# Expert stages: rows turned three groups ahead of the first products, second products two groups behind, one pipeline over both halves

## The reference

```python
x = hidden_states.reshape(-1, H)                       # 4096 tokens, H = 128
probs = jax.nn.sigmoid(x @ router_w.T + expert_bias)   # 160 experts
top_w, top_idx = jax.lax.top_k(probs, 8)               # 8 experts for each token
top_w = top_w / (jnp.sum(top_w, axis=-1, keepdims=True) + 1e-09) * 2.5
combine = zeros(T, 160).at[arange(T)[:, None], top_idx].set(top_w)
h1 = jax.nn.silu(einsum('th,eih->eti', x, w_gate))     # 128 -> 64 for each expert
routed = einsum('eti,ehi->th', h1 * combine.T[:, :, None], w_down)   # 64 -> 128
shared = jax.nn.silu(x @ w_gate_shared.T) @ w_down_shared.T
return routed + shared
```

## Time and profile before

| | |
|---|---|
| runs | 2842.09, 2843.34, 2848.13 us, median 2843.34 |
| span of the profiled execution (no other time of that execution is recorded) | 2871.3 us |
| PE busy | 2020.4 us (70%) |
| DVE, ACT, POOL busy | 1647.2, 1083.0, 1349.4 us |
| expert stage m: first `up` to last `take_y` | about 931 to 1288 us |
| expert stage n: the same | about 2307 to 2654 us, then gathers to the end |

### The profile page before, as it was taken

One profiled execution on the slowest core, in us unless ns is written; L12 is line 12 of the kernel. 1 busy time (PEld: TensorE's weight loads), 2 busy tenths in 40 slices (PEclk: granted clock), 3 DMA queues, 4 the chain that ended last, 5 costly groups with the idle time before them and its releaser, 6 DMA issues. The chain is left out here.

```text
span 2871.3 us, 44772 instructions
## 1 busy us (share of the span) xinstructions
PE 2020.4 (70%) x15403; PEld 1129.8 (39%) x15403; DVE 1647.2 (57%) x4701; ACT 1083.0 (38%) x2067; POOL 1349.4 (47%) x1372
## 2 busy tenths in 40 slices
PE   5898887887883775665887889888888467766000
PEld 3456455455461554541332333333332255545000
DVE  5457585775777231456776778778783533145222
ACT  0263453444541443340545543443444144443000
POOL 0043166566673444553445531641554444355775
PEclk9899989889995887775777877876876589787555
DMA  9200001000034664554131121121100656565221
GB/s 370 96 1 4 1 6 34 23 11 33 20 130 155 192 206 155 180 180 121 28 88 48 46 76 25 53 69 36 49 29 25 250 179 207 176 188 174 70 60 44
DMA packets 132471, 275.63 MB, mean 96 GB/s; under 512 B 29411, under 2 KB 44387, under 8 KB 127891
## 3 DMA queue, kind: packets, MB, share of 16 engines
q1 hardware_dynamic: 99478, 205.60, 21.7%
q0 software_dynamic: 32768, 67.17, 7.7%
HBM read 146.34 MB, written 125.93 MB: 95 GB/s over the span
## 5 line engine op out<-in xcount | busy, mean ns | idle before, releaser
L1473 POOL DMA_INDIRECT slots_in<-g_xs,g_place x512 | 510.1, 996 | 373.0 <-issue 122.7
L2518 ACT ACTIVATE b_pT<-b_psE 128x512 f32<-128x512 f32 (+3 forms) x768 | 325.6, 491 | 449.6 <-PE b_psE L2415 392.6
L2271 DVE TENSOR_REDUCE b_peak<-b_psM 128x1 f32<-128x512 f32 (+3 forms) x768 | 395.1, 551 | 148.6 <-PE b_psM L2403 91.3
L1498 POOL DMA_INDIRECT r_xs<-slots_out,g_place x336 | 333.3, 992 | 237.2 <-ACT b_pT L2518 98.3
L2400 PE MATMUL b_psM<-b_kS,b_qS 72*128 72x512 bf16 (+3 forms) x768 | 290.1, 412 | 60.6 <-DVE b_peak L2271 29.7
L2415 PE MATMUL b_psE<-b_qS,b_kS 75*128 75x512 bf16 (+3 forms) x768 | 250.5, 402 | 45.0 <-ACT b_pT L2518 38.6
L1498 POOL DMA_INDIRECT g_xs<-slots_out,g_place x176 | 173.0, 983 | 126.1 <-issue 48.0
L2060 DVE COPY m_staged_w<-wgd 128x192 f32 x512 | 98.3, 264 | 230.0 <-PE m_psY L2002 165.7
L2427 PE MATMUL b_psV<-b_pT,b_vb 128*32 128x512 f32 (+3 forms) x1536 | 205.8, 616 | 30.8 <-POOL b_pT L2582 29.5
L2060 DVE COPY n_staged_w<-wgd 128x192 f32 x512 | 97.5, 263 | 216.0 <-PE n_psY L2002 118.6
L2400 PEld LDWEIGHTS b_psM<-b_kS,b_qS 72*128 72x128 bf16 x768 | 84.5, 112 | 263.7 <-DVE b_peak L2271 151.6
(11 more groups left out here) (639 smaller groups left out, 4167.9 us busy)
## 6 DMA issues: line engine op xcount, KB each, us to landing
wgd<-in_w_gdT SPq DMA_DIRECT2D x8, 3840.0 KB, 22.7
slots_in<-g_xs SPq DMA_DIRECT2D x26, 1024.0 KB
m_rows<-slots_in SPq DMA_DIRECT2D x104, 256.0 KB
slots_out<-m_y SPq DMA_DIRECT2D x104, 256.0 KB
n_rows<-slots_in SPq DMA_DIRECT2D x104, 256.0 KB
slots_out<-n_y SPq DMA_DIRECT2D x104, 256.0 KB
b_qS<-q_parts SPq DMA_DIRECT2D x48, 192.0 KB
b_kS<-k_parts SPq DMA_DIRECT2D x48, 192.0 KB
```

The costliest lines, as they stand in the source:

```text
L1473: self.nc.gpsimd.indirect_dma_start(self.G.slots_in[self.h], bass.IndirectOffsetOnAxis(self.G.place[:, TPH * self.h + t, k:k + 1], 0), sel ...
L1498: self.nc.gpsimd.indirect_dma_start(self.rows(i)[:, k, :], None, self.G.slots_out[t // TPH], bass.IndirectOffsetOnAxis(self.G.place[:, t, ...
L2271: nc.vector.reduce_max(to, taking()[:, 0:size], AX.X).then_inc(m_taken, 1)
L2518: nc.scalar.activation(pT[:, e % KEPT, h, q0:HALF], psE[:, j % BANKS, q0:HALF], ACT.Exp, scale=SCALE).then_inc(e_taken, 1)
```

## The change

Only `experts` is touched, and both expert stages use it. New constants: `TURN_AHEAD = 3`, `DOWN_BEHIND = 2`, `HELD = 3`. One loop runs over the 104 groups of both halves. In step n PE does up(n), turn_rows(n+3), down(n-2), and ACT squash(n), take_xT(n+3), take_y(n-2). xT and hT get three buffers (HELD); the PSUM tiles keep two places. SP stores group n-2, then loads group n+7, as far as the transposes have freed a buffer; loads of half 1 begin at step 48 (`crossing`), the wait for its scatters stands before its first load. POOL's pace is taken from `hT_ready` in place of `y_ready`; the scatters are spread so that the last is released at group 46 of 52. The weights' staging on DVE and the sizes of all instructions are unchanged.

```diff
@@ SP
+            def load(n):
+                h, i = divmod(n, HALF_GROUPS)
+                if i == 0:
+                    for b in range(BPH * h, BPH * (h + 1)):
+                        sp.wait_ge(S.scattered[b], 16 * TPB * TOPK)
...
-            for h in range(HALVES):
-                for b in range(BPH * h, BPH * (h + 1)):
-                    sp.wait_ge(S.scattered[b], 16 * TPB * TOPK)
-                for i in range(DEEP):
-                    load(h, i)
-                for i in range(HALF_GROUPS):
-                    if i + DEEP < HALF_GROUPS:
-                        sp.wait_ge(x_turned, h * HALF_GROUPS + i + 1)
-                        load(h, i + DEEP)
-                    store(h, i)
+            loaded, crossing = DEEP, HALF_GROUPS - TURN_AHEAD - 1
+            for n in range(-TURN_AHEAD, GROUPS):
+                if n >= DOWN_BEHIND:
+                    store(n - DOWN_BEHIND)
+                for n_load in range(loaded, min(n + TURN_AHEAD + DEEP + 1, GROUPS if n >= crossing else HALF_GROUPS)):
+                    sp.wait_ge(x_turned, n_load - DEEP + 1)
+                    load(n_load)
+                    loaded = n_load + 1
+            for n in range(GROUPS - DOWN_BEHIND, GROUPS):
+                store(n)
@@ POOL
-                        pool.wait_ge(y_ready, first + done)
+                        pool.wait_ge(hT_ready, first + done)
...
-            spaced(scatter, TPH * TOPK - scatter.sent, 0, 3, 2)
+            left = TPH * TOPK - scatter.sent
+            spaced(scatter, left, 0, 3, lambda n: min(n // 3 * 2, n * (HALF_GROUPS - 2 * TURN_AHEAD) // left))
...
@@ PE
-            for h in range(HALVES):
-                first = h * HALF_GROUPS
-                turn_rows(first)
-                for i, (g, d) in enumerate(order):
-                    up(first + i, g, d, h * DYN_GROUPS)
-                    if i + 1 < HALF_GROUPS:
-                        turn_rows(first + i + 1)
-                    if i:
-                        down(first + i - 1, *order[i - 1])
-                down(first + HALF_GROUPS - 1, *order[HALF_GROUPS - 1])
+            for n in range(TURN_AHEAD):
+                turn_rows(n)
+            for n in range(GROUPS):
+                up(n)
+                if n + TURN_AHEAD < GROUPS:
+                    turn_rows(n + TURN_AHEAD)
+                if n >= DOWN_BEHIND:
+                    down(n - DOWN_BEHIND)
+            for n in range(GROUPS - DOWN_BEHIND, GROUPS):
+                down(n)
@@ ACT
-                if n >= 2:
-                    act.wait_ge(up_done, n - 1)
-                nc.scalar.activation(xT[:, n % 2, :], psX[:, n % 2, :], ACT.Copy).then_inc(xT_ready, 1)
+                if n >= HELD:
+                    act.wait_ge(up_done, n - HELD + 1)
+                nc.scalar.activation(xT[:, n % HELD, :], psX[:, n % 2, :], ACT.Copy).then_inc(xT_ready, 1)
```

More of the change, by code:

```diff
@@ L67 @@
 STAGED = 4
+TURN_AHEAD = 3
+DOWN_BEHIND = 2
+HELD = 3
 RING = 4
@@ L1946, in _, with spaced @@
         def _(pool):
-            def spaced(issue, count, first, transfers, groups):
+            def spaced(issue, count, first, transfers, groups_at):
                 for n in range(0, count, transfers):
-                    done = min(n // transfers * groups, HALF_GROUPS)
+                    done = groups_at(n)
                     if done:
-                        pool.wait_ge(y_ready, first + done)
+                        pool.wait_ge(hT_ready, first + done)
                     issue(min(transfers, count - n))
-            spaced(scatter, TPH * TOPK - scatter.sent, 0, 3, 2)
+            left = TPH * TOPK - scatter.sent
+            spaced(scatter, left, 0, 3, lambda n: min(n // 3 * 2, n * (HALF_GROUPS - 2 * TURN_AHEAD) // left))
             for s in S.scattered[BPH:]:
@@ L1959, in _ @@
                 pool.wait_ge(s, 16 * HALF_GROUPS // DEEP)
-            spaced(lambda count: gather.issue(pool, count), min(TPH, gather.tiles) * TOPK, HALF_GROUPS, 2, 1)
+            spaced(lambda count: gather.issue(pool, count), min(TPH, gather.tiles) * TOPK, HALF_GROUPS, 2,
+                   lambda n: min(n // 2, HALF_GROUPS))
             if out is not None:
@@ L1979, in turn_rows, with up @@
                 last.then_inc(x_turned, 1)
-            def up(n, g, d, ahead):
+            def up(n):
+                h, i = divmod(n, HALF_GROUPS)
+                g, d = order[i]
                 pe.wait_ge(xT_ready, n + 1)
@@ L1985, in up @@
                 if d is not None:
-                    pe.wait_ge(staged, ahead + d + 1)
-                elif n < HALF_GROUPS and GROUP * g % CHUNK == 0:
+                    pe.wait_ge(staged, h * DYN_GROUPS + d + 1)
+                elif h == 0 and GROUP * g % CHUNK == 0:
                     pe.wait_ge(S.weights_landed[GROUP * g // CHUNK], 16)
@@ L2036, in take_y @@
                                      psY[:, n % 2, :, 0:2 * DM].rearrange("p j (q d) -> p j q d", d=DM), ACT.Copy).then_inc(y_ready, 1)
-            for h in range(HALVES):
-                first = h * HALF_GROUPS
-                take_xT(first)
-                for n in range(first, first + HALF_GROUPS):
-                    squash(n)
-                    if n + 1 < first + HALF_GROUPS:
-                        take_xT(n + 1)
-                    if n > first:
-                        take_y(n - 1)
-                take_y(first + HALF_GROUPS - 1)
+            for n in range(TURN_AHEAD):
+                take_xT(n)
+            for n in range(GROUPS):
+                squash(n)
+                if n + TURN_AHEAD < GROUPS:
+                    take_xT(n + TURN_AHEAD)
+                if n >= DOWN_BEHIND:
+                    take_y(n - DOWN_BEHIND)
+            for n in range(GROUPS - DOWN_BEHIND, GROUPS):
+                take_y(n)
         @block.vector
```

26 lines of the change are left out of this document (14 added, 12 removed).

## The result

The changed kernel took 2857.57 us (median of 13 runs, 2846.72 to 2873.20), the kernel before 2845.43 us (13 runs). The ratio is 1.005, with a 95% interval of 1.0036 to 1.0065: half a per cent slower, where 2704 us, 5% faster, had been predicted. The profiled execution has a span of 2870.5 us and took 2871.81.

The account below looks back on a forecast made before the run. Bound: a PE-ACT-PE chain of waits with signals late in POOL's bursts. Gains 60 + 65 + 17 less 3 for stage start and end, 139 us, took the 2871.3 span to 2732; medians run 28 lower: 2704 us, range 2615 to 2805.

Parts of the forecast that it names:

- What bounds the kernel: Expert halves: no engine full; a PE-ACT-PE chain of waits, signals 2.5 to 4.5 us late in POOL's indirect DMA bursts.
- The deeper order: Both halves: two steps hold one PE-ACT-PE round trip; 2.4 us a group taken in half 0, 2.9 in half 1.
- terms of 60 us for the halves 0: Halves 0 of both stages: 104 groups at 2.4 us in place of 2.98, a gain of 60 us.
- term of 65 for the halves 1: Halves 1 of both stages: 104 groups at 2.9 us in place of 3.52, a gain of 65 us.
- GpSimd's pace: POOL waits for hT(n) instead of y(n), an earlier point in the same count; charged at no cost.
- PE's wait for xT: Sign in the profile after: this wait should nearly vanish; an equal wait for hT or y would refute the forecast.
- One loop: Junction of half 0 and half 1: shorter waits for rows, gaining 14 us in m and 3 in n, together 17.
- Rival D: Half 0: bursts start mid-step on hT_ready and their 4.4 us hold stops the pipeline; 86 us slower, 2929; chance 0.09.
- Rival C: Only the junction gains, since signals are held as long as POOL issues; 14 us gained, 2829 us; chance 0.12.
- Rival E: No effect, within 0.2%: an unseen bound, and the junction waits for the same scatters; chance 0.04.
- Rival B: Half 1: DVE and POOL take turns, so it gains 16 us and not 65; total 2753 us; chance 0.05.
- The clock in the halves 1: Sign in the profile after: PE's granted clock in half 1, 0.78 to 0.81 before, should rise above 0.8.

Follow-up runs that it names:

- e2: Changed kernel with scatters issued one at a time instead of three and half 1's gather pace begun eight groups later; ratio to the kernel before 0.9834.
- e12: Changed kernel with half 1's gathers in bursts of eight for every four groups, pace begun eight groups later; ratio to the kernel before 1.0165.
- e6: e2 with bursts of exactly two issues, each followed by three small GpSimd memsets that wait for each other; ratio to the kernel before 0.9852.
- e9: Changed kernel with GpSimd's pace taken from y_ready again instead of hT_ready; ratio to the kernel before 0.9953.
- e1: Changed kernel with TURN_AHEAD = 1, DOWN_BEHIND = 1, HELD = 2: one loop, old order of a step; ratio to the kernel before 1.0174.
- e4: Changed kernel with a GpSimd memset of 128 x 1152 fp32 in place of each gather, the gathers coming last; ratio to the kernel before 1.0728.
- e3: Changed kernel with half 0's gathers issued only after half 1's last store, DVE's adds after the staging; ratio to the kernel before 1.0257.
- e15: Changed kernel with plain GpSimd DMAs of the same 64 KB where the gathers stood, the gathers coming last; ratio to the kernel before 1.0364.
- e14: Changed kernel with gathers moving 256 bytes a row in place of 512, same number of issues; ratio to the kernel before 1.0079.
- e5: Changed kernel with half as many product matmuls a group, each wider, odd-placed experts left out; ratio to the kernel before 0.9821.

## Why the prediction was wrong

- **What bounds the kernel.** Right that no engine is full and that the lost time lies in GpSimd's bursts, and that signals come late, but incomplete in what happens there. I took "the late hand-overs" for late signals of a TensorE that goes on working. The sign that its stream stops too stood beside them in the timeline of PE in the kernel before, second products that break off after 13 matmuls and go on after an idle time that no engine ended:

```profile
1003.36 0.81 PE L2002 MATMUL m_psY<-m_staged_w,m_hT 64*64 64x128 f32 x13
1004.48 0.46 PE L2002 MATMUL m_psY<-m_staged_w,m_hT 64*64 64x128 f32 x3 [0.31 <-issue]
```

- **The deeper order.** This is the step that failed: "two steps hold one round trip", priced at 2.3 us a group with a lateness of 2.5 us, and 3.3 with 4.5. The price took the lateness as fixed and TensorE as working meanwhile. In the changed kernel a signal came up to 12.4 us late, and TensorE itself took 16.4 us for one step of 1.80; two steps of depth cover neither. The terms of 60 us for the halves 0 and 17 for the junctions came out as 33 together (8 + 25), the term of 65 for the halves 1 as -37.
- **GpSimd's pace, costed at nothing** ("cost or gain within the lateness above"). The loss grows with the burst (e2, e12, e6), and the change made bursts longer: permits from hT_ready (e9 without them has a mean of 4.0 and a longest of 8), a deeper order (4.6 and 10 without it, e1), and no pause between the halves, so that the gathers began with 14 in a row. Mean bursts in half 1 went from 2.9 to 6.0 issues in m, the longest from 6 to 14. The chain of waits shows it as ACT waiting for "remote" up to 7.2 us at a time in half 1 of m (1110 to 1270 us), where 4.6 was the longest before:

```profile
ACT m_hT L2043 <- remote: 48.4, 12, 7.2
PEld m_psH L2004 <- issue: 35.3, 67, 1.8
...
POOL r_xs L1501 <- DVE g_x L1528: 23.8, 4, 7.3
PE m_psH L2004 <- issue: 23.3, 31, 1.2
```

 As I had written, PE's wait for xT vanished; an "issue" wait with no engine behind it took its place.
- **One loop.** The mechanism was right, 3.3 us of wait for rows in place of 15.3 in m and 3.2 in place of 5.0 in n, but the pause that it removed had kept the gathers from running in arrears with the pace from hT_ready (first burst of half 1 in m 14 issues, before 2).
- **Rival D** (a burst starts in the middle of a step and its hold isn't hidden) has the right place, GpSimd's wait on hT_ready, and the right sign; but the loss fell on half 1, which it left unchanged, and half 0 gained, and the whole was 12 us slower, not 86. **Rival C** (GpSimd's holds set the period, 14 us faster) has the right engine and the wrong sign. **Rival E** (no effect) is nearest in size, and the measured ratio of 1.0036 to 1.0065 lies just outside its 0.2%; its ground, a bound not seen and a junction that waits as before, isn't what happened.
- **Rival B and the Trainium skill's rule** (SBUF — State Buffer, "Who interferes with whom") would need DVE and GpSimd to take turns. For indirect DMAs they don't (in e12 eight copies took 1.68 us from 1162.14 with nearly all of one gather's issue, 1162.11 to 1163.06, and part of the next beside them), for memsets they do (e4).
- The clock in the halves 1 didn't rise above 0.8; it was 0.75 with TensorE standing, and 1.00 where it was kept busy (e3).

Open: why the issue of an indirect DMA holds TensorE up, and whether its work or only its signals and its next instructions are held. It needs the indirect form (e15), isn't the number of bytes (e14), isn't GpSimd being busy (e4), and goes little by the count of TensorE's instructions (e5). How the index reads or the writing of descriptors could reach TensorE was not tried apart. Every execution of the experiments has a recorded span and clock, so none ran without recording, and that the recording has a part in it is not excluded. No run leaves out the scatters of half 0, so that they cost TensorE what gathers do is inferred from the same signs in the trace.

The medians differ by 12 us, the two profiled executions by less than one (2871.3 and 2870.5 us). In these two the expert stages differ by +9 us in m and -5 in n, and the other stages, which are the same code, by the rest (stage m begins at 931 and at 921 us; from m's last y to n's first products are 1019 and 1025 us). So the halves show where the change gains and loses, but not the median's 12 us to the microsecond.

## What to carry to other kernels

Before a pipeline is made deeper against late signals, look at the sender's own records, and at what sets how late the signals are. Where the records thin out into ones and threes with unexplained "issue" gaps, and the lateness grows with another engine's burst, the deeper order was worth 0.8 to 1.2% here, and the length of the bursts decided the rest. In this kernel it paid to pace GpSimd's indirect DMAs so that they don't fall into arrears beside matmuls, in bursts of two with a pause of about 1 us, and to let them run freely only where they are the last thing left. When a pace moves to an earlier signal, work out how many permits can pile up.

## What was not expected of the hardware

- While GpSimd issued 16 indirect DMAs back to back, TensorE took 16.4 us for a step of 1.80 us, with the DMA engines busy 0.40 of the time, and its signals came up to 12.4 us after the matmuls' records. A plain DMA of the same size from GpSimd costs next to nothing (half 1 of m 101 us against 95 without any, 0.07 us each), an indirect one 0.6 to 1.2 us.
- By the records of that burst the stop begins only some 3 us after the first issue of a burst (2459.96 to 2463.4) and ends up to 2.7 us after the last (2479.90 to 2482.60); by the half times 0.7 to 2 us of each burst are free.
- Four GpSimd memsets of 1.17 us each stretched eight fp32 copies on DVE from 1.5 to 5.7 us.
